# A four-layer gated cross-attention stack on one core: the first layer's output, two norms, quantised layer and first queries cut into two chains by batch

## The reference, cut to what matters

```python
x = x + tanh(g_xattn[0]) * L0_xattn(ctx, ctx, layernorm(x), ...)   # windows of keys and values, sampled
x = x + tanh(g_ffn[0])   * L0_ffn(layernorm(x), rhs)               # 8-bit quantised product
x = x + tanh(g_xattn[1]) * L1_xattn(layernorm(x), ctx, ctx, ...)   # 16 heads of 8, softmax over 1024 keys
x = x + tanh(g_ffn[1])   * L1_ffn(layernorm(x), ...)               # mixture of 8 experts
...                                                                # two more layers in the same manner

def L0_ffn(lhs, rhs):
    lhs_scale = max(absmax(lhs, row), 1e-12) / 127;  rhs_scale = max(absmax(rhs, column), 1e-12) / 127
    q_lhs, q_rhs = clip(round(lhs / lhs_scale), -127, 127), clip(round(rhs / rhs_scale), -127, 127)
    return (q_lhs @ q_rhs) * lhs_scale * rhs_scale
```

## Time and profile before

| | us |
|---|---|
| three runs, median (lowest to highest) | 1199.7 (1192.54 to 1201.85) |
| the profiled execution, its own time | 1195.01 |
| its span, first to last instruction | 1193.3 |
| PE busy in the span | 1063.0 |
| DVE busy in the span | 781.8 |
| mean granted clock of PE, 1 being 2.4 GHz | 0.915 |

### The profile page before, as it was taken

How to read it: one execution, slowest core, us unless ns; L and a number is a source line. 1 busy time by engine, 2 the same in 40 slices (tenths; PEclk the granted TensorE clock), 3 DMA queues, 4 the chain that set the end, 5 groups by cost and what they waited for, 6 DMA issues and landing times.

```text
span 1193.3 us, 17122 instructions
## 1 busy us (share of the span) xinstructions
PE 1063.0 (89%) x6458; PEld 601.6 (50%) x6458; DVE 781.8 (66%) x1444; ACT 484.9 (41%) x715; POOL 214.3 (18%) x258
## 2 busy tenths in 40 slices
PE   8798858999989868998799999997989997999998
PEld 4333423444434447994344444444778786344445
DVE  4979675888888241443688886843545554688616
ACT  2562311477757601110147764672311211067452
POOL 2666312111111011003211111100300401111000
PEclk9799877799999968999869999999999999689799
DMA  8599602013310505982412231100343340100011
GB/s 255 165 296 341 219 0 87 11 32 110 119 57 12 160 27 164 357 313 63 145 48 54 55 104 31 42 2 36 106 162 121 124 145 2 30 11 12 1 28 36
DMA packets 79572, 121.81 MB, mean 102 GB/s; under 512 B 10125, under 2 KB 53296, under 8 KB 79482
## 3 DMA queue, kind: packets, MB, share of 16 engines
q1 hardware_dynamic: 59782, 79.41, 21.6%
q10 hardware_dynamic: 18932, 39.10, 9.4%
q0 software_dynamic: 768, 2.10, 0.5%
HBM read 92.45 MB, written 27.81 MB: 101 GB/s over the span
## 4 chain that ended last, share of the span: by engine, by line
PE 56%; DVE 21%; issue 4%; ACT 2%; POOL 2%; DMA 2%; SPq 0%; DVEq 0%; ACTq 0%; POOLq 0%
DVE arena L2046 14%; PE bank L1408 11%; PE bank L1368 11%; PE bank L1586 10%; PE st_bank L1514 3%; PE bank L1526 3%; PE st_bank L1393 3%; PE st_bank L1586 2%; DVE xn L1697 2%; PE st_bank L1336 2%; PE bank L1438 1%; PE bank L1374 1%; PE st_bank L1177 1%; DVE bnst L1677 1%; PE bank L1380 1%
## 5 line engine op out<-in xcount | busy, mean ns | idle before, releaser
L2046 DVE TENSOR_REDUCE arena<-bank 128x1 f32<-128x512 f32 x640 | 400.3, 685 | 67.9 <-PE bank L1368 67.8
L1073 ACT ACTIVATE arena<-st_bank 128x1024 f32<-128x1024 f32 x320 | 315.9, 1022 | 157.2 <-PE st_bank L1393 156.0
L1368 PE MATMUL bank<-g_a 64*128 64x512 f32 x480 | 184.7, 518 | 12.3 <-DVE arena L2046 2.9
L1408 PE MATMUL bank<-arena,vaug 128*9 128x256 f32 (+2 forms) x2560 | 175.3, 393 | 1.7 <-ACT arena L1073 1.7
L1368 PEld LDWEIGHTS bank<-g_a 64*128 64x128 f32 x480 | 75.8, 200 | 122.3 <-DVE arena L2046 83.8
L1586 PE MATMUL bank<-g_a,g_w 128*128 128x512 f32 x512 | 117.6, 390 | 4.3 <-DVE g_w L2248 3.2
L1393 PE MATMUL st_bank<-g_a 64*128 64x512 f32 x480 | 116.5, 443 | 0.0
L1586 PEld LDWEIGHTS bank<-g_a,g_w 128*128 128x128 f32 x512 | 95.8, 188 | 25.4 <-DVE g_w L2248 3.6
L1408 PEld LDWEIGHTS bank<-arena,vaug 128*9 128x9 f32 (+2 forms) x2560 | 56.6, 93 | 80.4 <-issue 43.4
L1368 PE MATMUL bank<-g_x,g_a 64*128 64x512 f32 x160 | 64.3, 525 | 9.2 <-DVE arena L2046 3.2
L849 POOL CAST arena<-arena 8x128 fp32r<-8x128 f32 x40 | 11.4, 285 | 308.8 <-ACT arena L1066 308.8
(11 more groups left out here) (299 smaller groups left out, 1468.4 us busy)
## 6 DMA issues: line engine op xcount, KB each, us to landing
arena<-in_glu_w SPq DMA_DIRECT2D x39, 512.0 KB, 3.3
arena<-kv_table SPq DMA_DIRECT2D x11, 1024.0 KB, 8.1
ctxT<-in_glu_w ACTq DMA_DIRECT2D x22, 512.0 KB, 6.5
arena<-in_w SPq DMA_DIRECT2D x20, 512.0 KB, 6.2
kparts<-arena ACTq DMA_DIRECT2D x12, 512.0 KB, 5.4
arena<-in_w ACTq DMA_DIRECT2D x12, 512.0 KB, 3.4
xnT<-kv_table SPq DMA_DIRECT2D x5, 1024.0 KB, 7.5
g_a<-kparts SPq DMA_DIRECT2D x24, 192.0 KB
```

Source lines behind the costliest of these rows:

```text
L1073: act.activation(prob[sl % PROBS], st_bank[sl % 2][:], ACT.Exp, scale=scale).then_inc(exp_ready, 1)
L1368: pe.matmul(bank[TURN_BANKS[place % 3]], Qc[gi % KQ_BUFS][rows, hh, qt * P:(qt + 1) * P], Kc[gi % KQ_BUFS][rows, half * CH:(half + 1) * CH ...
L1408: ins = pe.matmul(bank[7][at:at + dh + 1, 0:D], vaug[l][:, b * KT + 2 * m + i, h0 + hh, :], tiles[:, a], start=(m == 0 and i == 0), stop=( ...
L2046: dve.tensor_reduce(mxh[gi % 2][:, col, hf:hf + 1], bank[TURN_BANKS[place % 3]], AX.X, ALU.max).then_inc(max_red, 1)
```

## The change

SP: the gates' loads go ahead of the rest of the context; the second batch's context is loaded behind window 1, the later keys' weights behind window 3; the wait for x ahead of the attention loads goes. Entry on DVE: `sample_mod(0)` ahead of block 4, `sample_points(0)` ahead of block 5, `coverage(0)` from behind turn 0 to behind `sample_points(1)`. Entry on ScalarE: copies and stores of blocks 6 to 8 alternate with the weights of tiles 1 to 3; on PE block 6 goes ahead of the second offsets.

The output uses two banks a batch with two tiles each, a bias product for a whole bank ahead of the products, and its statistics, norm, quantising and quantised product are run batch by batch, the second batch's output behind the first's quantising. The queries of batch 0 are made before the second batch's quantised product; tokens and queries of batch 1 follow inside attention 1, after maxima 3, 7 and 10. ScalarE fills the attention buffers, between the two context copies. The 7 hold products ahead of the tokens go, the 30 behind the queries become 16.

The diff, cut (removed bodies are in the functions above; changes for the second copy of the turns, which isn't run, and bodies that only moved are left out):

```diff
...
-LN_HOLDS = {2: 7, 3: 8, 4: 60, 5: 22, 6: 12, 7: 16}
-QUERY_HOLDS = {1: 30, 2: 20, 3: 22}
+LN_HOLDS = {3: 8, 4: 60, 5: 22, 6: 12, 7: 16}
+QUERY_HOLDS = {1: 16, 2: 20, 3: 22}
...
+OUT0_BANKS = (6, 4)
+TOKENS_AT_MAX, QUERY_AT_MAX, SPLIT_AT_MAX = 3, 7, 10
...
+            if l == 1 and u in (TOKENS_AT_MAX, QUERY_AT_MAX, SPLIT_AT_MAX):
+                steps.append((("late tokens", "late query", "late split")[(TOKENS_AT_MAX, QUERY_AT_MAX, SPLIT_AT_MAX).index(u)],))
...
+        def out0(t):
+            return bank[OUT0_BANKS[t // QT] + t % QT // 2][:, t % 2 * D:(t % 2 + 1) * D]
...
-            ld(ctxT[:, :, 3 * P:M - P], ctx_in[:, :, 3 * P:M - P], ld_ctx[0])
-            ld(ctxT[:, :, M:2 * M], ctx_in[:, :, M:2 * M], ld_ctx[1])
...
-            for l in ATT:
...
+            ld(ctxT[:, :, 3 * P:M - P], ctx_in[:, :, 3 * P:M - P], ld_ctx[0])
...
+                if t == 1:
+                    ld(ctxT[:, :, M:2 * M], ctx_in[:, :, M:2 * M], ld_ctx[1])
+                if t == QT - 1:
+                    for l in ATT:
+                        ld(a_wk[l], rows(io[f"wk{l}"]), ld_prep)
+                    ld(a_wv, rows(io["wv"]), ld_prep)
+                    for l in (2, 3):
+                        ld(a_bk[l][0:min(EW[l], P)], io[f"bk{l}"], ld_prep)
...
-            sp.wait_ge(x_ready, 2 * NT)
...
-                pool.wait_ge(x_ready, 2 * l * NT)
...
+                if l > 1:
...
-            def ctx_evac(l, width):
...
+            def ctx0_evac(b):
+                act.wait_ge(prod_ready, 2 * NT - 1)
+                for c in range(DC):
+                    act.wait_ge(ctxT_mm, b * DC + c + 1)
+                    act.activation(xnT[:, c, b * CH:(b + 1) * CH], bank[b * DC + c], ACT.Copy).then_inc(ctxT_ready, 1)
...
+            act.wait_ge(u_ready, 1)
+            row_weights(0)
...
-            act.wait_ge(u_ready, 1)
-            for t in range(QT):
-                row_weights(t)
...
-            kv0_copy(6)
...
+            for n in range(3):
+                kv0_copy(KV_FIRST + n)
+                kv0_store(KV_FIRST + n)
+                row_weights(1 + n)
...
-            ctx_evac(0, D)
+            ctx0_evac(0)
+            for i in range(PBUFS):
+                act.wait_ge(prep_st[i], 16 * PARTS * (KCHUNKS // PBUFS))
+            act.wait_ge(ctxn_ready, 2 * NT)
+            act.wait_ge(zero_ready, 1)
+            act.wait_ge(kq_clear, 1)
+            for g in range(KQ_BUFS):
+                if g:
+                    act.activation(Kc[g], bc(onesf[:, 0:1], [P, M]), ACT.Copy)
+                act.activation(Qc[g], bc(zero_row[:, 0:1].unsqueeze(2), [P, HG, CH]), ACT.Copy).then_inc(kq_clear, 1)
+                if g == 1:
+                    ctx0_evac(1)
...
-            def i8_evac():
...
+            act.wait_ge(i8_bc, 1)
+            act.activation(i8sc_bc, bank[OUT0_BANKS[0]][:, 0:D], ACT.Copy).then_inc(i8_qT, 1)
+            def i8_tokens_evac(b):
+                for c in range(DC):
+                    act.wait_ge(i8_tr, DC * (b + 1) + c + 1)
+                    act.activation(i8xT[:, c, b * CH:(b + 1) * CH], bank[b * DC + c][:, 0:CH // 2].bitcast(BF16), ACT.Copy).then_inc(i8_qT, 1)
...
+            def query_part(l, j):
...
+                q_store(l, k, 0)
...
-                for j in range(QCH0[l + 1] - QCH0[l]):
...
+                if l > 1:
...
-                    if step[0] == "turn":
+                    if step[0] == "late tokens":
+                        ln_evac(2, [1])
+                    elif step[0] == "late query":
+                        query_part(1, 1)
+                        q_store(1, 1, 1)
+                    elif step[0] == "turn":
...
-            ln_evac(2)
+            i8_tokens_evac(0)
+            ln_evac(2, [0])
+            query_part(1, 0)
+            q_store(1, 0, 1)
+            i8_tokens_evac(1)
...
-            def project_out(stage, wmat, width, bias, l):
...
+            pe.wait_ge(ld_bkv, 16)
+            kv0_products(6, 7)
...
-            pe.wait_ge(ld_bkv, 16)
-            kv0_products(6, 12)
+            kv0_products(7, 12)
...
+            pe.wait_ge(prepv_evac, NCT)
+            def out0_products(b):
+                pe.wait_ge(ctxT_ready, (b + 1) * DC)
+                for t in range(b * QT, (b + 1) * QT):
+                    for c in range(DC):
+                        ins = pe.matmul(out0(t), xnT[:, c, t * P:(t + 1) * P], wo0[:, c, :], start=False, stop=(t % 2 == 1 and c == DC - 1))
+                    if t % 2:
+                        ins.then_inc(out_mm, 2)
+            def out0_bias(b):
+                for i in range(QT // 2):
+                    pe.matmul(bank[OUT0_BANKS[b] + i], onesf[0:1, :], bc(bo0[:].unsqueeze(1), [1, 2, D]), start=True, stop=False)
+            transposes(ctx0, ctxT_mm, 0, D, ctxn_ready, 0, [0])
+            out0_bias(0)
+            out0_products(0)
...
-            pe.wait_ge(prepv_evac, NCT)
-            transposes(ctx0, ctxT_mm, 0, D, ctxn_ready, NT)
-            project_out(0, wo0, D, bo0[:], 0)
+            transposes(ctx0, ctxT_mm, 0, D, ctxn_ready, 0, [1])
+            out0_bias(1)
...
-            pe.wait_ge(x_ready, NT)
+            out0_products(1)
+            pe.wait_ge(x_ready, QT)
...
-                ins = pe.matmul(bank[4][:, i * P:(i + 1) * P], bc(i8wsc[:, i:i + 1], [P, P]), ident[:], start=True, stop=True)
+                ins = pe.matmul(bank[OUT0_BANKS[0]][:, i * P:(i + 1) * P], bc(i8wsc[:, i:i + 1], [P, P]), ident[:], start=True, stop=True)
...
-            for t in range(NT):
...
+            def i8_transposes(b):
+                pe.wait_ge(i8_qT, DC)
+                for t in range(b * QT, (b + 1) * QT):
+                    pe.wait_ge(i8_xq, t + 1)
+                    for c in range(DC):
+                        ins = pe.transpose(bank[b * DC + c][:, 0:CH // 2].bitcast(BF16)[:, (t % QT) * P:(t % QT + 1) * P], i8xq[:, t, c * P:(c + 1) * P], identb[:])
+                        if t % QT == QT - 1:
+                            ins.then_inc(i8_tr, 1)
+            def i8_products(b):
+                pe.wait_ge(i8_qT, DC + 1 + (b + 1) * DC)
+                pe.wait_ge(x_ready, QT * (b + 1))
+                for t in range(b * QT, (b + 1) * QT):
+                    for c in range(DC):
+                        ins = pe.matmul(out0(t), i8xT[:, c, t * P:(t + 1) * P], i8wT[:, c, :], start=(c == 0), stop=(c == DC - 1))
+                    if t % 2:
+                        ins.then_inc(out_mm, 2)
+            i8_transposes(0)
+            i8_products(0)
...
+            def query_product(l, j):
...
-                for j in range(QCH0[l + 1] - QCH0[l]):
...
+                if l > 1:
+                    for j in range(QCH0[l + 1] - QCH0[l]):
+                        query_product(l, j)
+                    hold_clock(QUERY_HOLDS[l], 4)
+                else:
+                    hold_clock(QUERY_HOLDS[l], 1)
+                    pe.wait_ge(x_ready, stage * NT)
...
+                    elif step[0] == "late tokens":
+                        ln_transposes(2, [1])
+                    elif step[0] == "late query":
+                        query_product(1, 1)
...
-            hold_clock(LN_HOLDS[2], 2)
-            ln_transposes(2)
+            ln_transposes(2, [0])
+            query_product(1, 0)
+            i8_transposes(1)
+            i8_products(1)
...
-            def add_out(stage, tg, banks=4):
...
-            steps_ps = [bank[3 - b][:, 0:half] for b in range(B)]
+            steps_ps = [bank[i][:, 0:half] for i in (3, 1)]
...
+            sample_mod(0)
...
-            sample_mod(0)
+            sample_points(0)
...
-            sample_points(0)
...
-                    dve.tensor_reduce(ctx0[:, n - NT, :], by_row(a_prod[n % 2]), AX.X, ALU.add).then_inc(ctxn_ready, 1)
+                    summed = dve.tensor_reduce(ctx0[:, n - NT, :], by_row(a_prod[n % 2]), AX.X, ALU.add)
+                    if uncovered:
...
+                    else:
+                        summed.then_inc(ctxn_ready, 1)
...
-            coverage(0)
...
+            coverage(0)
...
-            add_out(0, tgx[:, 0:1])
...
+            def add_out0(b):
+                for t in range(b * QT, (b + 1) * QT):
+                    dve.wait_ge(out_mm, t - t % 2 + 2)
+                    dve.scalar_tensor_tensor(x[:, t, :], out0(t), tgx[:, 0:1], x[:, t, :], ALU.mult, ALU.add).then_inc(x_ready, 1)
+                    if t % QT:
+                        tile_statistics(1, t - 1)
+                tile_statistics(1, (b + 1) * QT - 1)
+            def quantise(b):
+                tiles = slice(b * QT, (b + 1) * QT)
+                dve.wait_ge(xn_ready, NT + (b + 1) * QT)
+                ch.link(dve.tensor_reduce(i8xsc[:, tiles], xn[:, tiles], AX.X, ALU.max, apply_absolute_value=True))
...
+                for t in range(b * QT, (b + 1) * QT):
+                    ins = dve.tensor_scalar(xn[:, t], xn[:, t], i8xr[:, t:t + 1], MAGIC, ALU.mult, ALU.add)
+                ch.link(ins)
```

(33 more changed lines are left out.)

169 lines of the change are left out of this document (51 added, 118 removed).

## The result

The changed kernel takes 1191.4 us in the median of 17 runs, the kernel before, on the same chip, 1199.05 us in 17: a ratio of 0.9932, 95% interval [0.9912, 0.9952]. That is 8 us where 18 were forecast. When both were timed a second time, the ratio was 0.9967 [0.9944, 0.9990]: 4 us. The direction held; the median stands at the upper edge of the range (1171 to 1192 us); the size did not hold.

The account below looks back on a forecast made before the run. Bound: a chain between engines, none full, from window work to the first maximum. Stretch 18.8 less 2.3 given back is 16.5, plus entry 1.5: 18 us off the median 1199.7, about 1182 us; range 1171 to 1192.

Parts of the forecast that it names:

- Entry: Start of the kernel: DVE's 4.41 us wait for the fifth window goes; gain 1.5 us, bounds 0.2 and 4.6.
- the second coverage is done at about 58.7 us: Entry, on DVE: the second coverage ends at about 58.7 us, against 61.3 us in the kernel before.
- Output stretch: End of window work to attention 1's first row maximum: 44 us instead of 62.8, 18.8 us less.
- the slow normalisation: Second half of the last normalisation, 4.05 us beside POOL's fills against 1.35 for the first: 2.7 us come back.
- waits only for the second pair of tiles: Start of the output stretch: DVE waits 0.7 us for output products, PE needing 1.06 us a tile.
- the wait for the first query chunk: Output stretch: DVE waits 0.8 us for the first query chunk, its product taking 2.9 us at the low clock.
- Given back in attention: Attention 1: late query product, split and late transposes cost 2.3 us together (1.8 to 2.8).
- The signs it named: Profile after: first maximum near 181 us, DVE share 0.8; wrong if past 190 us or clock 0.5 over 20 us.
- Rival 1: Entry gives 4.6 us instead of 1.5, attention starts warm: 21 to 24 us gained, about 1177; chance 0.14.
- Rival 2: Output stretch: the two chains only half overlap; gain 8 to 11 us, about 1190; chance 0.12.
- Rival 3: Attention 1 stays at the low clock, up to 10.7 us more a group; three cold groups 1214 us; chance 0.04.
- Rival 4: Something unseen keeps attention at its old place and waits only change names: 1198 us; chance 0.04.

Follow-up runs that it names:

- after: The changed kernel as it stands, first timing and profile: 1191.4 us, ratio 0.9932 to the kernel before.
- after_again: The changed kernel, unchanged, timed and profiled a second time: ratio 0.9967 to the kernel before.
- entry_only: The kernel before with only the new entry order added: 1198.09 us, ratio 1.0009 to the kernel before.
- fills_pool: The changed kernel with the seven buffer fills moved from ScalarE back to POOL, at the earliest place: 1190.16 us, ratio 0.9952 to the kernel before.
- pause: The changed kernel with 14 further chained weight reductions on DVE ahead of the output stage: 1195.19 us, ratio 0.9981 to the kernel before.
- sum_mid: The changed kernel with PE's coverage sum between the second and third of the last four key-value products: 1184.35 us, ratio 0.9890 to the kernel before.
- output_again: The changed kernel with its entry put back to the old order, run a second time: ratio 0.9901 to the kernel before.
- sum_mid_again: The changed kernel with the coverage sum between the second and third of the last four products, run again: 1184.73 us, ratio 0.9871 to the kernel before.

## Why the prediction was right and wrong, point by point

*Entry: forecast +1.5 us, bounds 0.2 and 4.6; measured -5.2 in the profiles (-2 to -8), about -3.5 by the times. This is the step that failed.* Its mechanism was right: the 4.41 us wait goes, PE stands idle before the coverage sum, comes out at the low clock, and all behind hangs on it. What was wrong is mainly one time, "the second coverage is done at about 58.7 us": it is done at 62.8 to 63.8. Four warm products behind it (2.97 us each from the sum's start) would end at 75.4 us in the mean, and in the kernel before they end at 75.3: of the 4.6 us that the entry had to give, nothing was there. That is 4.7 of the 6.7 us between forecast and profiles.

The rest is the clock. Start to start a product takes 2.97 us warm. In after one of the four took 5.03 us, in after_again two took 5.72 and 4.34, in entry_only three took 5.71, 5.72 and 4.84 (the fourth begins at 80.19 us). The four lost 2.1 us in after, 4.1 in after_again, 4.6 in fills_pool, 7.2 in pause and 7.4 in entry_only, mean 5.1. The prediction's 4.4 us (4.2 when its rows, too, are taken start to start) was near that mean, but it came from one recovery, behind a wait of 3.12 us, and stood as a bound. And the forecast took 1.5 us where that row left 0.2. With the coverage where it was, the term's range was about -7 to 0, an estimate from these five profiles.

The Trainium skill (TensorE: Matmul & The Clock Gate, "Part 1: The HAM clock gate (the "warmup" mystery)") says that the number of slow matmuls at a kernel's start varies from run to run. The traces show the same in the middle of a kernel: behind waits of 7.2 to 8.6 us one product ran low in after, two in after_again and three in entry_only.

*Output stretch: forecast 18.8 us, measured 14.5* (mean of three profiles of the old form 62.1 us, of nine of the new 47.6). In after DVE's work was right to 0.2 us, the 2.7 us of the slow normalisation came back (1.38 us for 4.05), and the deviations (forecast 1.6, measured 1.55) and the wait behind ScalarE's stores (2.6, measured 2.73) were right to 0.1. The fills took 1.04 to 1.06 us, where I took 1.15, and were hidden. Mis-sized was the start, "waits only for the second pair of tiles: 0.7 us": 2.1 us in the first profile, 1.2 to 4.3 in the others. The stage began 2.1 us late and ScalarE handed the first half over 0.9 us behind its start, 0.7 forecast, so that was nearly right. PE's first output products were not at 1.06 us a tile:

```profile
140.67 1.08 ACT L910 ACTIVATE xnT<-st_bank 128x512 f32<-128x512 f32 x2 [2.89 <-issue]
141.81 5.41 PE L1311 MATMUL bank<-wo,xnT 128*128 128x256 f32 x16 [0.96 <-ACT xnT L910]
```

The clock was 0.65 between 142 and 144 us and 0.50 between 144 and 146; the second batch's same products took 3.67 us at 1.00. ScalarE's last key store was issued until 140.6 us, and the copy stood behind it; in sum_mid and output_again PE's bias products, at the low clock, ended after the copy, and the store cost nothing. The low clock of the first outputs stood in the prediction only as a bound of the gain. Mis-sized too was the wait for the first query chunk, 0.8 us forecast and 2.08 measured. PE at 1.2 GHz in the second half of this stretch [the window 167 to 180 us had a clock of 0.50] made the query product 3.78 us where I had 2.9.

*Given back in attention: forecast 2.3 us (1.8 to 2.8), measured 3.7* (16.97 us from first maximum to first score in three profiles of the old form, 20.7 in nine of the new). The product held PE for 3.54 us and not 1.9 to 2.9; DVE's wait was 3.0 and not 0.6 to 1.6. PE ran at 0.50 there (188 to 192 us); the prediction's upper figure was the low clock too, 2.9 us, taken as half of the 5.82 us that ran partly warm.

Sum of what was measured: 14.5 - 3.7 - 5.2 = 5.6 us, and 7.1 with the entry's -3.7 of the three profiles near their medians. The two timings gave 8.2 and 3.9.

*The signs it named.* The first maximum came at 187.4 us in after, ahead of the limit of 190, but at 191.4 in after_again, behind it. DVE's busy share of the stretch was 0.75, not 0.8; no wait on a bias product was left; the line forecast near 75.5 us (L1953 before, L2002 here) came at 78.85, behind ScalarE and with PE idle before its sum, as written.

*Rivals.* Rival 1's 4.6 us in the entry exist: they need the sum two products later (136.1 against 138.8 gives 2.7 of them). Rival 2 had the number, "about 1190", and part of the reason, the low clock in the stretch; but more than half of the loss lies in the entry. Rival 3 did not occur: the clock was 0.51 from 200 to 218 us, where before it was 0.50 from 206 to 226, and 0.98 between 220 and 400 us (0.97 before). No run changes the number of holds alone. Rival 4 did not occur.

## What to carry to other kernels

When a wait is taken from one engine, follow the next in-order queue: here a one-column matmul stood ahead of four long products, and its place decided 8 us, more than the mean of the change's two timings (6 us). Before counting on a gain, work out when the last input of that small instruction is ready: here it was 4 us later than assumed, and the gain was gone. Bound the cost of an idle TensorE by several executions, not by one recovery. And give a helper engine's copies, for which somebody waits, precedence over its DMA issues, for which nobody does: that took 1.4 to 1.7 us from one wait here.

## What the runs showed of the hardware

Executions of one kernel differ by more than the changes made here, and the mean granted clock goes with it: the changed kernel's 17 runs reach from 1183.1 us at a clock of 0.916 to 1197.5 at 0.907. In 23 runs of the kernel before (those beside sum_mid_again) a thousandth of mean clock goes with 0.75 us (correlation -0.8); in the three other such sets with 0.4 to 0.8 us (-0.7 to -0.9). A single profile's tail from the first score to the end was between 973.2 and 983.7 us for reasons that no edit here touched, so a stage is better judged by its own length in several profiles than by the span of one.

The granted clock can stay low although PE has work without a pause: in entry_only it was 0.50 from 63.9 to 79 us while PE was busy all the time, and in after 0.51 from 200 to 218 us with PE busy for 17.5 of 18 us.
